# A Swin block: the second MLP layer in half precision, and x loaded a step ahead in two tiles

## The reference, cut to what matters

```python
B, H, W, C = 32, 56, 56, 128; HEADS, WS, SS = 16, 7, 3; HD = 8; HID = 512   # float32
y = _ln(x, norm1_g, norm1_b); y = jnp.roll(y, (-SS, -SS), axis=(1, 2))       # shifted 7x7 windows, 49 tokens
qkv = yw @ qkv_w.T + qkv_b
attn = softmax(einsum('bhqd,bhkd->bhqk', q * scale, k) + bias + mask)
o = einsum('bhqk,bhkd->bhqd', attn, v) @ proj_w.T + proj_b
x = shortcut + roll_back(o)
h = _ln(x, norm2_g, norm2_b)
h = gelu(h @ fc1_w.T + fc1_b)
return x + (h @ fc2_w.T + fc2_b)
```

## Time and profile before

| | value |
|---|---|
| median of three runs | 4095.21 us |
| the profiled execution, its own time | 4095.41 us |
| span of the profiled execution | 4093.6 us |
| mean granted TensorE clock (share of full speed) | 0.995 |
| TensorE matmuls busy | 3947.3 us (96%) |
| VectorE busy | 2855.1 us (70%) |
| ScalarE busy | 2674.9 us (65%) |
| GpSimd busy | 2002.3 us (49%) |

### The profile page before, as it was taken

The page is one execution under the profiler, slowest core; times in us unless marked ns, Lnnn a source line. Parts: engine busy times, 40 slices in busy tenths (PEclk is TensorE's granted clock), DMA queues, the critical chain, the costliest instruction groups (busy, mean ns, idle before and its releaser), DMA issues. The chain is left out here.

```text
span 4093.6 us, 168809 instructions
## 1 busy us (share of the span) xinstructions
PE 3947.3 (96%) x72080; PEld 3111.1 (76%) x72080; DVE 2855.1 (70%) x7453; ACT 2674.9 (65%) x3712; POOL 2002.3 (49%) x3476
## 2 busy tenths in 40 slices
PE   3899999999999999999999999999999999999998
PEld 2677777777777777777777777777777777777776
DVE  6677677677767777776776776777777667677764
ACT  1666666666666666666766666666666666666664
POOL 4454545445455454544544544454454445445453
PEclk8999999999999999999999999999999999999999
DMA  2333333333333333333333333333333333333332
GB/s 77 100 108 115 109 109 112 110 105 112 114 106 110 113 111 110 111 113 105 112 114 105 110 114 110 109 111 108 108 109 117 106 109 112 112 105 109 112 109 60
DMA packets 609568, 441.49 MB, mean 108 GB/s; under 512 B 142083, under 2 KB 608371, under 8 KB 608819
## 3 DMA queue, kind: packets, MB, share of 16 engines
q1 hardware_dynamic: 608355, 428.88, 35.6%
q0 software_dynamic: 464, 1.81, 0.2%
HBM read 106.14 MB, written 51.46 MB: 38 GB/s over the span
## 5 line engine op out<-in xcount | busy, mean ns | idle before, releaser
L589 DVE TENSOR_REDUCE neg_max<-ps 113x16 f32<-113x784 f32 x1024 | 995.9, 973 | 760.7 <-PE ps L741 760.5
L421 ACT ACTIVATE probs<-ps 113x784 f32<-113x784 f32 x1024 | 844.6, 825 | 858.4 <-PE ps L776 855.7
L821 PE MATMUL ps<-w,hid 128*112 128x128 f32 x7168 | 933.5, 279 | 1.9 <-ACT hid L438 1.0
L821 PEld LDWEIGHTS ps<-w,hid 128*112 128x112 f32 x7168 | 818.4, 177 | 81.9 <-issue 79.4
L776 PE MATMUL ps<-st_q,st_k 128*49 128x196 f16 x8192 | 696.2, 249 | 0.0
L771 PE MATMUL ps<-bias,eye_k 106*64 106x392 f16 x4096 | 686.5, 331 | 0.0
L438 ACT ACTIVATE hid<-ps,col 128x784 f32<-128x784 f32 x512 | 468.1, 915 | 165.4 <-PE ps L805 144.2
L741 PE MATMUL ps<-mx_k,mx_q 128*49 128x196 f16 x8192 | 544.2, 253 | 31.7 <-DMA mx_q<-q_hi 20.0
L350 POOL TENSOR_SCALAR ve<-mv 112x7 f32<-112x7 f32 x256 | 54.4, 212 | 1048.4 <-DVE mv L527 903.1
L776 PEld LDWEIGHTS ps<-st_q,st_k 128*49 128x49 f16 x8192 | 446.9, 105 | 122.0 <-issue 0.5
L372 POOL TENSOR_SCALAR r_hi<-sums 128x98 f16<-128x98 f32 x128 | 36.5, 285 | 897.9 <-DVE sums L630 897.9
(11 more groups left out here) (109 smaller groups left out, 6502.4 us busy)
## 6 DMA issues: line engine op xcount, KB each, us to landing
st_k<-k_hi SPq DMA_DIRECT2D x256, 196.0 KB
st_q<-q_hi SPq DMA_DIRECT2D x1024, 49.0 KB
oT_raw<-pv_sb SPq DMA_DIRECT2D x256, 196.0 KB, 3.6
x_in<-in_x SPq DMA_DIRECT2D x224, 196.0 KB
x_res<-in_x SPq DMA_DIRECT2D x224, 196.0 KB
out_y<-y_out SPq DMA_DIRECT2D x224, 196.0 KB
mx_k<-k_hi SPq DMA_DIRECT2D x512, 49.0 KB
mx_q<-q_hi SPq DMA_DIRECT2D x128, 196.0 KB
```

The lines of the kernel that those rows point to most:

```text
L421: nc.scalar.activation(probs[0:KP, w % 4, :].rearrange("p (b c) -> p b c", b=2), ps[0:KP, b:b + 2, 0:HB * WT], ACT.Exp).then_inc(s_exp, 1)
L589: nc.vector.tensor_reduce(neg_max[0:KP, :, :, w].rearrange("p e g -> p g e"), ps[0:KP, 0:2, :].rearrange("p b (g c) -> p (b g) c", g=2)[:, ...
L821: last = mm(ps[0:TP, 7, (i - first) * C:(i - first + 1) * C], hid[:, c, i * TP:(i + 1) * TP], w_2[:, c, :], start=(c == 0), stop=(c == CH ...
```

## The change

`fc2` takes `hid` and `w_2` as pairs of half-precision tiles, `hid_hi`, `hid_lo`, `w2_hi`, `w2_lo`, with 12 matmuls for a token tile in place of 4 in float32. The gelu writes its float32 result into the tile of the exponentials (`hid = probs`), VectorE rounds it to `hid_hi` (four copies a step), GpSimd makes `hid_lo` (four subtractions), and the exponentials of w = 0 to 3 wait for `hid_lo` of their chunk. `finish` divides by the scale of the weights. x_in becomes two tiles, loaded for unit t+3; the statistics are made in the attention loop at w = 4 to 6 and aggregated at the end of the body. The bias on x_res moves ahead of r_hi on GpSimd. The second v copy goes from VectorE to ScalarE, after the first exponential. The set-up scales and splits `w_2`.

```diff
--- before.py
+++ after.py
-        w_2 = sb("w_2", [C, CH, C])
+        w2_hi, w2_lo = (sb(n, [C, CH, C], F16) for n in ("w2_hi", "w2_lo"))
-        x_in = sb("x_in", [TP, WS, C])
+        x_in = [sb(f"x_in{e}", [TP, WS, C]) for e in range(2)]
-        hid = sb("hid", [C, CH, WS * TP])
+        hid_hi, hid_lo = (sb(n, [C, CH, WS * TP], F16) for n in ("hid_hi", "hid_lo"))
+        hid = probs
+        w_2 = pv_sb[:, :, :].rearrange("p g q -> p (g q)")[:, 0:CH * C].rearrange("p (a n) -> p a n", a=CH)
...
@@ SyncE, body @@
-                n = t + 2
-                if exists(n) and n != 0:
-
-                    sp.wait_ge(s_t1, n)
-                    band_dmas(sp, xr, x_in, n, edge(n), False, s_x)
+                n = t + 3
+                if exists(n):
+
+                    sp.wait_ge(s_st1, n)
+                    if past(n, 1):
+                        sp.wait_ge(s_t1, n - 1)
+                    band_dmas(sp, xr, x_in[odd(3)], n, edge(n), False, s_x)
...
@@ GpSimd, body @@
                 n = t - 1
                 if exists(n):
 
+                    if n == 0:
+                        pool.wait_ge(s_w, 16 * N_W)
+                        pool.wait_ge(s_init, 2)
+                    pool.wait_ge(s_xres_dma, loads(n, edge(n)))
+                    nc.gpsimd.tensor_tensor(x_res[:, :, :], x_res[:, :, :],
+                                            proj_b[:, :].unsqueeze(1).to_broadcast([TP, WS, C]),
+                                            ALU.add).then_inc(s_xres, 1)
                     pool.wait_ge(s_rsum, n + 1)
...
-                    if n == 0:
-                        pool.wait_ge(s_w, 16 * N_W)
-                        pool.wait_ge(s_init, 2)
-                    pool.wait_ge(s_xres_dma, loads(n, edge(n)))
-                    nc.gpsimd.tensor_tensor(x_res[:, :, :], x_res[:, :, :],
-                                            proj_b[:, :].unsqueeze(1).to_broadcast([TP, WS, C]),
-                                            ALU.add).then_inc(s_xres, 1)
...
+                n = t - 2
+                if exists(n):
+                    for c in range(CH):
+                        pool.wait_ge(s_hid_hi, CH * n + c + 1)
+                        nc.gpsimd.tensor_tensor(hid_lo[:, c, :], hid[:, c, :], hid_hi[:, c, :],
+                                                ALU.subtract).then_inc(s_hid_lo, 1)
...
@@ ScalarE @@
+                if w < CH and exists(n - 2):
+                    act.wait_ge(s_hid_lo, CH * (n - 2) + w + 1)
...
             def gelu(n, c):
-                if c == 0 and past(n, 0):
-                    act.wait_ge(s_fc2, 2 * n)
...
                         exp_pair(t, w)
+                        if w == 0:
+                            nc.scalar.activation(v_place(0, 1), v_made(0, 1), ACT.Copy).then_inc(s_vown_b, 1)
...
@@ VectorE @@
+            then(nc.vector.tensor_scalar(w_2, w_2, W_SCALE, None, ALU.mult))
+            then(nc.vector.tensor_copy(w2_hi[:, :, :], w_2))
+            then(nc.vector.tensor_tensor(w2_lo[:, :, :], w_2, w2_hi[:, :, :], ALU.subtract))
...
+                nc.vector.scalar_tensor_tensor(
+                    y_out[:, i0:i1, :], ps[0:TP, 7, 0:(i1 - i0) * C].rearrange("p (i c) -> p i c", c=C),
+                    1 / W_SCALE, x1_b[:, i0:i1, :], ALU.mult, ALU.add).then_inc(s_fin, 1)
+
+            def hid_high(n, c):
+                dve.wait_ge(s_gelu, CH * n + c + 1)
+                if c == 0 and past(n, 0):
+                    dve.wait_ge(s_fc2, 2 * n)
+                nc.vector.tensor_copy(hid_hi[:, c, :], hid[:, c, :]).then_inc(s_hid_hi, 1)
...
                     finish(t - 3, 0, edge)
-                n = t + 2
-                if exists(n) and n != 0:
-                    norm1(n, edge)
+                if exists(t - 2):
+                    hid_high(t - 2, 0)
+                    hid_high(t - 2, 1)
...
+                if exists(t - 2):
+                    hid_high(t - 2, 2)
+                    hid_high(t - 2, 3)
                 n = t
...
-                n = t
-                if exists(n):
-                    dve.wait_ge(s_v, 2 * n + 2)
-                    nc.vector.tensor_copy(v_place(0, 1), v_made(0, 1)).then_inc(s_vown, 1)
...
+                    n = t + 3
+                    if exists(n):
+
+                        if w == 4:
+                            dve.wait_ge(s_x, loads(n, edge(n)))
+                            stats(x_in[odd(3)], st1, (0, 1))
+                        if w == 5:
+                            stats(x_in[odd(3)], st1, (1, 4))
+                        if w == 6:
+                            stats(x_in[odd(3)], st1, (4, WS)).then_inc(s_st1, 1)
                 if exists(t - 2):
                     finish(t - 2, 1, edge)
+                if exists(t + 3):
+                    moments1(t + 3)
...
@@ TensorE, fc2 @@
-                    pe.wait_ge(s_gelu, CH * (n + 1))
+                    pe.wait_ge(s_hid_hi, CH * (n + 1))
...
+                row = ps[0:TP, 7, (i - first) * C:(i - first + 1) * C]
                 for c in range(CH):
-                    last = mm(ps[0:TP, 7, (i - first) * C:(i - first + 1) * C], hid[:, c, i * TP:(i + 1) * TP], w_2[:, c, :],
-                              start=(c == 0), stop=(c == CH - 1))
+                    for w_part in (w2_hi, w2_lo):
+                        mm(row, hid_hi[:, c, i * TP:(i + 1) * TP], w_part[:, c, :],
+                           start=(c == 0 and w_part is w2_hi), stop=False)
+                for c in range(CH):
+                    if i == first and p == 1:
+                        pe.wait_ge(s_hid_lo, CH * n + c + 1)
+                    last = mm(row, hid_lo[:, c, i * TP:(i + 1) * TP], w2_hi[:, c, :], start=False, stop=(c == CH - 1))
```

More of the change, by code:

```diff
@@ L109, in swin_block_kernel @@
         nm1, nm2 = sb("nm1", [TP, WS]), sb("nm2", [TP, WS])
-        z1, z2 = x_in, sb("z2", [TP, WS, C])
+        z2 = sb("z2", [TP, WS, C])
         yT_hi, yT_lo = ([sb(f"{n}{e}", [C, NW, 2, HP], F16) for e in range(2)] for n in ("yT_hi", "yT_lo"))
@@ L157, in swin_block_kernel @@
          s_xres_dma, s_xres, s_x1, s_st2, s_ln2, s_ve2, s_rs2, s_mr2, s_nm2, s_z2, s_x1b, s_t2, s_h_hi,
-         s_h_lo, s_fc1, s_gelu, s_fc2, s_fin, s_stored, s_bd1, s_bd2, s_zero, s_init, s_initp, s_inita, s_bt,
+         s_h_lo, s_fc1, s_gelu, s_hid_hi, s_hid_lo, s_fc2, s_fin, s_stored, s_bd1, s_bd2, s_zero, s_init, s_initp, s_inita, s_bt,
          s_bv, s_bp_mm, s_vown_b, s_y_hi, s_y_lo, s_w_split) = (
@@ L169, in swin_block_kernel @@
                 "mean_rstd2_done", "neg_mean2_done", "z2_ready", "x1_biased", "z2_transposed",
-                "h_high_ready", "h_low_ready", "fc1_done", "gelu_done", "fc2_done", "y_ready", "y_stored",
+                "h_high_ready", "h_low_ready", "fc1_done", "gelu_done", "hid_high_ready", "hid_low_ready", "fc2_done", "y_ready", "y_stored",
                 "strips_out", "bias_in", "bias_cleared", "vector_set_up", "gpsimd_set_up", "scalar_set_up",
@@ L217, in _ @@
         def _(sp):
-            band_dmas(sp, xr, x_in, 0, False, False, s_x)
+            band_dmas(sp, xr, x_in[0], 0, False, False, s_x)
             for strips, table in ((strips_k, table_k), (strips_q, table_q)):
@@ L393, in body @@
                                             ALU.add).then_inc(s_x1b, 1)
+                n = t - 2
[4 more added lines that the diff above has]
+                                                ALU.subtract).then_inc(s_hid_lo, 1)
                 n = t + 2
                 if exists(n):
-                    norm(n, s_ln1, mv1, ve1, s_ve1, rs1, s_rs1, mr1, s_mr1, nm1, s_nm1, x_in, z1, s_t1, s_z1)
+                    norm(n, s_ln1, mv1, ve1, s_ve1, rs1, s_rs1, mr1, s_mr1, nm1, s_nm1, x_in[odd(2)], x_in[odd(2)], s_t1, s_z1)
                 n = t - 1
@@ L528, in aggregate, with moments1 @@
                 last.then_inc(s_mv, 1)
-            def norm1(n, edge):
-                dve.wait_ge(s_x, loads(n, edge(n)))
+            def moments1(n):
                 if past(n, 0):
                     dve.wait_ge(s_z1, n)
-                stats(x_in, st1, (0, WS)).then_inc(s_st1, 1)
                 aggregate(n, st1, s_st1, mv1, s_ln1)
             nc.vector.memset(hid[:, 0:2, :], 0.0).then_inc(s_zero, 1)
-            norm1(0, lambda n: False)
+            dve.wait_ge(s_x, loads(0, False))
+            stats(x_in[0], st1, (0, WS)).then_inc(s_st1, 1)
+            moments1(0)
             nc.vector.memset(bv_wide, 0.0)
@@ L580, in finish @@
                 dve.wait_ge(s_fc2, 2 * n + 2 - p)
-                nc.vector.tensor_tensor(y_out[:, i0:i1, :],
-                                        ps[0:TP, 7, 0:(i1 - i0) * C].rearrange("p (i c) -> p i c", c=C),
-                                        x1_b[:, i0:i1, :], ALU.add).then_inc(s_fin, 1)
+                nc.vector.scalar_tensor_tensor(
[6 more added lines that the diff above has]
+                nc.vector.tensor_copy(hid_hi[:, c, :], hid[:, c, :]).then_inc(s_hid_hi, 1)
             def row_maxima(n, w):
@@ L782, in pv @@
                 if u == 0:
```

(12 more changed lines are left out.)

## The result

The changed kernel takes 4039.04 us in the median (4037.15 to 4044.04), beside 4093.22 us for the kernel before in the same comparison. The ratio is 0.9867, with a 95% interval of 0.9849 to 0.9885: 1.3% faster. The forecast was 4036 us, so it was right. The profiled execution took 4044.04 us, the longest of the four (span 4042.2, mean granted clock 0.992).

A forecast was written before the change was run, and what follows sets the result against it. TensorE bounds the kernel, with VectorE's chain nearly as long in the head. 30.64 + 0.75 - 0.95 + 0.1, say 30.56 us a step against 31.05: 62 us less, 3 more, gives 4036 us; 8 in 10 range 3925 to 4240.

The forecast's parts named there:

- TensorE's gain: fc2 matmuls 0.056 us apart in half precision: 0.60 us less in the head, 0.95 us gained in the loop.
- The third rival: fc2's matmuls of 112 columns don't keep 0.056 us; at 0.109 us the step is 33.9 us, 4460 us; chance 0.08.
- My estimate of 4300 us: The whole kernel if fc2's matmuls cost 0.093 us, the skill's load price for 112 columns.
- The port: In the head, the second cast waits for GpSimd's bias on x1; k_lo starts at 2010.25, the head is 0.75 us longer.
- hid_lo and the sum of the chain: In the head, each hid_lo takes 1.83 us on GpSimd; x1 ends at 2016.8 and max_logits starts at 2016.9.
- the wait that I gave the third cast: In the head, VectorE's third cast waits for the second hid_lo and ends at 2014.3; 0.2 us of waiting.
- The edits costed at nothing: Loop hid_lo, v copy on ScalarE, statistics at w = 4 to 6, norms and DMAs add nothing to the step.
- The mean: Mean step of 30.56 us against 31.05, with 0.1 us kept for a late mx_q.
- the 0.41 us of the kernel before: Excess of the mean step, 31.05 us, over the shown 30.64; put down to late DMAs, mostly x_in's load.
- Set-up and tail: +3 us for set-up vector steps, a last hid_lo chain in the tail, and first steps not waiting for x_in.
- No port cost: In the head, casts run as soon as the gelus end; step 29.75 us, 166 us less, 3932 us; chance 0.15.
- The lock-out: In the head, the second cast waits for bias on x1 and first hid_lo, until 2012.1; 4250 us; chance 0.22.

The follow-up runs named there:

- xb_split: The changed kernel with GpSimd's bias on x1 in two pieces, four token tiles ahead of r_hi and three behind r_lo; 4092.92 us, ratio 0.9996.
- vcopy_back: The changed kernel with the second v copy back on VectorE, behind x1; 4044.95 us, ratio 0.9882.
- xres_back: The changed kernel with the bias on x_res put back behind r_lo on GpSimd, ahead of the bias on x1; 4692.96 us, ratio 1.1468.
- cast_reduce: The changed kernel with the first two casts written as a reduction over an axis of one element; 3949.87 us, ratio 0.9658.
- x_only: The kernel before with only the x_in part: two tiles, load for t + 3, statistics at w = 4 to 6; 4076.14 us, ratio 0.9964.
- split_pair: xb_split with hid_lo of a chunk waiting for both casts of its pair; 3960.51 us, ratio 0.9684.

## Why the prediction was right, point by point

**TensorE's gain: right.** The matmuls of `fc2` stand 0.056 us apart, as I took it (in the head of the shown step the first starts at 2012.13 and `fc1`, 36 matmuls later, at 2014.14), though their loads are 131 ns where those of 128 columns are 98:

```profile
L855 PEld LDWEIGHTS ps<-w_hi,hid_hi 128*112 128x112 f16 x3584 | 420.1, 131 | 84.5 <-issue 79.6 <-DVE hid_hi L604 3.8 <-DVE y_out L596 1.1
...
2004.71 0.22 PE L855 MATMUL ps<-w_lo,hid_hi 128*112 128x128 f16 x1
2004.77 0.22 PE L855 MATMUL ps<-w_hi,hid_hi 128*112 128x128 f16 x1
2004.82 0.22 PE L855 MATMUL ps<-w_lo,hid_hi 128*112 128x128 f16 x1
```

So the load is slower at 112 columns than at 128, and it costs nothing, since it lies under the matmuls. The loop fell by 0.99 us (forecast 0.95). The third rival is out. (The Trainium skill, "TensorE: Matmul & The Clock Gate", section "Weight-path perf modes — Fast Weight Load (FWL) and DoubleRow", has the faster load for 128 columns only, and the trace agrees on the order: 98 against 131 ns. The 93 ns for 112 columns, from the section "LDWEIGHTS (loading the stationary operand)" of the same page of the Trainium skill, are not what was measured, 131 ns. My estimate of 4300 us took that load as the spacing of the matmuls, and that did not come.)

**The port: right, and the step that carries the rest.** Forecast: second cast ends with the bias on x1, at 8.8 us behind the transposes of z; measured 8.95. k_lo 8.73 against 8.87, v projection 11.0 against 11.14, first `max_logits` 15.38 against 15.23. One detail was wrong: the first cast does not wait for r_lo. It starts 0.02 us before it, and r_lo waits: 649 ns on the mean in place of 0.28 us.

**hid_lo and the sum of the chain: 0.2 us too high.** I took 1.83 us, by elements. Free of a cast hid_lo takes 1.67 us, as in xb_split; the page's mean of 1817 ns has waits for casts in it. So the wait that I gave the third cast did not come: the second hid_lo ends at 2022.75, just as oT does. The two casts end at 2022.71 + 1.03 = 2023.74, 13.11 us behind the transposes of z, where I had 13.18. x1 ends at 2025.72, 1.98 us later, where I had 2.1 for the v copy and x1; in the records each of VectorE's instructions starts some 0.1 us before the last has ended. The two more than made up for the 0.14 us by which k_lo came later.

**The edits costed at nothing: right for the v copy** (vcopy_back) **and for the loop's statistics** (loop 15.01 us in quick steps). The move of the bias on x_res was costed only as a GpSimd time that starts earlier. xres_back shows that it keeps the third and fourth casts clear of the first three hid_lo, and that 654 us hang on it.

**The mean: two terms wrong, in opposite directions.** I kept 0.1 us for late DMAs over the shown step of 30.44 us. The shown step is 30.25 us and the mean 0.32 above it. TensorE waits 32.9 us for mx_q, 0.26 a step, more than in the kernel before (20.0 us); in some of these steps x1 would have held it for 0.20 us anyway. Two more waits have grown, from 2.0 and 1.5 us:

```profile
PE ps L919 <- DMA r_rows<-r_lo: 11.4, 12, 2.3
PE ps L823 <- issue: 9.6, 18, 1.1
```

The second is in the attention product, where the profile shows nothing that TensorE waits for; its cause is open. It is part of why the loop is 15.18 us on the mean against 15.02 in the shown step. mx_q is issued 12.38 us behind the transposes of z on the mean, against 11.97 in the kernel before and 12.17 in cast_reduce. That r_lo, whose transfer stands ahead of it in SyncE's queue, ends some 0.4 us later fits a part of this, but was not tested in this kernel. I had put the 0.41 us of the kernel before mostly on x_in; x_only shows that a quarter to a half of it was. The -0.19 and the +0.22 cancel. A mean step of 30.57 us against a forecast of 30.56 is therefore partly luck. So is the last 0.02 us of that forecast, for which I gave no reason (the terms add up to 30.54).

**Set-up and tail:** +9.7 us against +3. The tail has no attention loop under which hid_lo lies.

**The rivals.** No port cost: excluded by the 2.30 us cast, and rebuilt by cast_reduce. The lock-out: not in this kernel, but it is real (xb_split, xres_back). I had priced 1.8 us at the second cast with 214 us (4250 against 4036); between xb_split and split_pair 1.6 us at that cast are worth 132 us. What I wrote against it, that a cast of 512 elements got in after one piece, is no rule. Nor is my reading that a waiting cast goes ahead of the next instruction, on which the forecast rests: it held for the second cast of this kernel, and that it did there was in part luck.

## What to carry to other kernels

Where VectorE copies or casts from SBUF to SBUF while GpSimd works, look at what GpSimd has ready behind the running instruction, not only at that instruction: the same cast took 0.57, 1.22, 2.30, 2.85 or 3.66 us here. A form of the cast that needs no shared port can win although it is slower by itself. And once a chain has been shortened, read which DMA is issued last in its queue: here a transfer whose data had long been ready stood behind four others, and moving its issue to another engine brought 1%.

## What the runs showed of the hardware that I had not expected

- A cast that waits for the port may be passed by a whole ready instruction of GpSimd (xb_split: 2.85 us; xres_back, behind one that it already waited for: 3.66 us), or go ahead of it (changed kernel: 2.30 us). What decides was not settled.
- A half-precision weight load of 112 columns takes 131 ns, one of 128 columns 98 ns. Neither shows in the spacing of the matmuls, 0.056 us.
- One TensorE wait of 2.42 us in a step of 33 us was followed, about 1.6 us after work resumed, by matmuls at 0.11 us in place of 0.056; the mean granted clock was 0.96. Waits of 0.47 and 0.49 us in the changed kernel left it at 1.00 over 300 to 3800 us.
